# Two loops over groups unrolled into single streams of products, and rows of maxima moved in one transfer

## The chip, the cores and the metric

The kernel runs on one core of a Trainium2 chip. The metric is the device time of one execution in microseconds (us). Three runs of the kernel before took 4997.11, 5010.97 and 5019.95 us; the median is 5010.97 us.

## What is computed

The program is a chain of eight blocks over 4096 tokens of width 128 (16 sequences of 256), each with a residual and a layer norm: an encoder of six attention layers, a mixture of experts, a gated delta rule, an FP4 network, a linear attention, a ternary network, an attention with rotary positions, and a Fourier mix. The change touches the encoder, the experts, the ternary network and the rotary attention. Cut to what matters, the reference of the two networks is:

```python
# experts: every token goes through the shared network and all 8 experts; the gates are zero but for the top 2
shared = silu(x @ shared_w1.T) @ shared_w2.T                    # 128 -> 512 -> 128
logits = x @ gate_w.T                                           # 8 per token
gates  = scatter(softmax(top_k(logits, 2)))
expert_out = einsum('teh,edh->ted', silu(einsum('td,ehd->teh', x, experts_w1)), experts_w2)
out = shared + einsum('ted,te->td', expert_out, gates)          # then x + out, layer norm

# ternary network: _tlin(x, w, s) = (x @ w.T) * s, weights in {-1, 0, 1}
h = silu(_tlin(x, w1)) * _tlin(x, w2)                           # 128 -> 512
h = gelu(_tlin(h, h1)); h = gelu(_tlin(h, h2))                  # 512 -> 512, twice
out = _tlin(h, w3)                                              # 512 -> 128, then x + out, layer norm
```

In both attentions a softmax over 256 keys is taken for 16 heads of width 8. Its row maxima have to be known before the second pass over the scores; they are split into three bf16 pieces and enter that pass as three more rows of the product's operand.

## The kernel before, in words

The activations live in one array `H`, width on 128 partitions and 4096 tokens along it, worked in 8 groups of 512 tokens (`GROUP`, `GROUPS`). Blocks run one after another; each first loads its weights (`par_s<-par_in_s`). Every engine has its own stream of instructions, written out by hand in each block's `@block.tensor`, `.vector`, `.scalar`, `.gpsimd` and `.sync` function; semaphores join them, and nothing reorders them.

**Experts** (lines 1583 to 1723). All engines loop over the groups with `Fori`, so a group is begun when the last one is done. GpSimd copies the group from `H` to `cur` (L92). TensorE makes the 8 gate logits of each token (L1631, four small products), then for the shared network and each of 8 experts `up(e)` (L1640: four products of 512 columns into four banks) and `down(e)` (L1653: 16 products of 128 columns; for e = 0 four more, L1650, that add the residual by way of the identity), in the order up(0), up(1), down(0), up(2), down(1), ... down(8). ScalarE takes the SiLU of each `up` (L1717), VectorE adds each `down` with its gate (L1702). Then comes the norm, with a shared set of buffers: statistics on VectorE (L42 to L50), the root on GpSimd (L68), the scaling on VectorE (L56), four transposes on TensorE (L76, `norm_tensor`), the copy to `H` on ScalarE (L84), and with that the next round's copy to `cur`.

**Ternary network** (lines 2315 to 2403), likewise: per group 8 products for the two inputs' matrices (L2351, L2352), 16 and 16 for the two hidden layers (L2364), 4 for the output (L2368), all of 512 columns, then the residual and norm as above with four transposes more (L2372). ScalarE holds one table of functions at a time: it takes SiLU for the first four and GELU for the next eight activations of a group.

**Maxima.** In the encoder one sequence (`u`) is attended at a time, in four rounds T = 0 to 3 of four heads each. VectorE reduces the scores of sequence u + 2 (L751) while sequence u is in its second pass (scores L479, exponential L892, values L490). In round 2 of sequence u the maxima of u + 1 are turned by TensorE (L467) and copied by ScalarE to `turned_max`, 48 rows (three pieces by 16 heads) of 256 bf16 values (L881). The SyncE queue then runs `row_of_maxima`: it waits for that copy, stores `turned_max` to DRAM (L293), waits for the store (`s_nms`), and loads it back as three rows of 4096 values behind the query pieces (L295). TensorE waits for it (`s_nml`) before the first product of sequence u + 1 (L479). The same queue also stores the query and key pieces of the group after next (L286, L289), which ScalarE's queue waits for before it issues their loads (L263, L265). There are 96 such moves in the encoder and 16 in the rotary attention, where the lines are L1085 and L1087 and the product that waits is L1214.

Layer norms of the encoder and most blocks go through the class `Chain`, which has buffers of its own for each instance, and whose parts (`move`, `statistics`, `root`, `apply`, `turn`, `back`) are called apart.

## Time and profile before

| | |
|---|---|
| runs of the kernel before | 4997.11, 5010.97, 5019.95 us |
| profiled execution, its own time | 5029.85 us |
| its span, first to last instruction | 5027.8 us |
| TensorE matmul busy | 3880.8 us (77%) |
| TensorE weight load busy | 2644.1 us (53%) |
| VectorE busy | 2797.8 us (56%) |
| ScalarE busy | 1896.4 us (38%) |
| GpSimd busy | 786.3 us (16%) |
| mean granted TensorE clock | 0.861 |
| data moved by DMA | 224.83 MB, 45 GB/s |

The profiled execution ran 0.4% longer than the median of the runs. Busy shares are means over eight blocks with different limits; by time of the span the encoder lies at 0 to 2257 us, the experts at 2258 to 2878, the ternary network at 4219 to 4614, and the rotary attention from there to about 4970. The granted clock is the share of TensorE's full clock of 2.4 GHz that was let through: 1.00, or 0.50 at the lower level.

### The profile page before, as it was taken

The numbers are of one execution on the slowest core, as the hardware profiler recorded it, in microseconds if no ns is written. First come the engines' busy times: TensorE is split into PE (matmuls) and PEld (weight loads), VectorE is DVE, ScalarE is ACT, GpSimd is POOL, SyncE is SP. The second block draws the span as 40 slices with busy tenths as digits, with TensorE's granted clock in tenths as the row PEclk, the third lists the DMA queues.
The fourth block names the chain that finished last, engine by engine and source line by source line (L and its number), as shares of the span: only waits on it lengthen the run. The fifth ranks groups of instructions, "written<-read, shape, count | busy, mean of one in ns | idle before, by whom it ended". The sixth has DMA issues, their size and how long they took to land. (4 is left out here: it accounts for less than half of the span.)

```text
span 5027.8 us, 72866 instructions
## 1 busy us (share of the span) xinstructions
PE 3880.8 (77%) x27543; PEld 2644.1 (53%) x27543; DVE 2797.8 (56%) x6776; ACT 1896.4 (38%) x2957; POOL 786.3 (16%) x1074
## 2 busy tenths in 40 slices
PE   5898888888888888868898744477745566887986
PEld 3666666666666666656666511155423332333664
DVE  4756656746746647551212277788679773111663
ACT  2554554554545545533333233322212122221343
POOL 2212222222222122130000000000000031002221
PEclk8999999998999899988999866589857677998897
DMA  5414414423424324200000000000000000001431
GB/s 124 101 36 107 105 42 100 106 53 90 95 49 114 74 61 112 75 10 29 0 0 0 13 0 0 0 1 1 1 5 0 4 1 23 0 0 34 105 86 32
DMA packets 158830, 224.83 MB, mean 45 GB/s; under 512 B 17950, under 2 KB 138142, under 8 KB 141214
## 3 DMA queue, kind: packets, MB, share of 16 engines
q10 hardware_dynamic: 19656, 107.37, 9.7%
q1 hardware_dynamic: 138878, 113.45, 8.3%
q8 instruction: 193, 3.16, 0.3%
q14 instruction: 103, 0.84, 0.1%
HBM read 157.18 MB, written 63.57 MB: 44 GB/s over the span
## 5 line engine op out<-in xcount | busy, mean ns | idle before, releaser
L751 DVE TENSOR_REDUCE enc_mx<-psum 128x2 f32<-128x512 f32 (+1 forms) x1152 | 753.2, 686 | 408.4 <-PE psum L460 404.1
L892 ACT ACTIVATE enc_e<-psum 128x1024 f32<-128x1024 f32 (+1 forms) x768 | 580.7, 808 | 506.6 <-PE psum L479 446.5
L460 PE MATMUL psum<-enc_ks,enc_qs 80*128 80x128 bf16 (+1 forms) x3072 | 469.2, 259 | 126.0 <-DVE enc_mx L751 110.8
L479 PE MATMUL psum<-enc_qs,enc_ks 83*128 83x256 bf16 (+1 forms) x3072 | 393.2, 255 | 95.6 <-DMA enc_qs<-max_pieces 87.2
L460 PEld LDWEIGHTS psum<-enc_ks,enc_qs 80*128 80x128 bf16 x3072 | 224.6, 102 | 268.9 <-DVE enc_mx L751 174.6
L490 PE MATMUL psum<-enc_e,enc_v 128*32 128x256 f32 (+1 forms) x6144 | 347.7, 346 | 0.0
L479 PEld LDWEIGHTS psum<-enc_qs,enc_ks 83*128 83x128 bf16 x3072 | 263.1, 101 | 145.7 <-DMA enc_qs<-max_pieces 101.5
L1653 PEld LDWEIGHTS psum<-par_s,moe_act_h 128*128 128x128 f32 x2304 | 268.6, 192 | 26.8 <-issue 26.8
L1640 PE MATMUL psum<-cur,par_s 128*128 128x512 f32 x576 | 275.2, 625 | 0.0
L1717 ACT ACTIVATE moe_act_h<-psum 128x512 f32<-128x512 f32 x288 | 169.4, 598 | 273.5 <-PE psum L1640 272.9
L1653 PE MATMUL psum<-par_s,moe_act_h 128*128 128x128 f32 x2304 | 271.5, 275 | 0.0
L1702 DVE SCALAR_TENSOR_TENSOR moe_acc<-psum,moe_gates,moe_acc 128x128 f32<-128x128 f32 x256 | 72.1, 345 | 352.4 <-PE psum L1653 352.4
L490 PEld LDWEIGHTS psum<-enc_e,enc_v 128*32 128x32 f32 x6144 | 165.5, 112 | 170.6 <-ACT enc_e L892 53.3
L169 POOL TENSOR_TENSOR enc_n_rstd<-enc_n_vareps,minus_half 128x4 f32<-128x4 f32 x112 | 114.1, 1019 | 897.9 <-DVE enc_n_vareps L165 888.7
L2364 PE MATMUL psum<-ter_h,par_s 128*128 128x512 f32 x512 | 221.0, 592 | 0.0
L548 PE MATMUL psum<-par_layerr,enc_hidden 128*128 128x128 f32 x1536 | 211.3, 283 | 0.0
L548 PEld LDWEIGHTS psum<-par_layerr,enc_hidden 128*128 128x128 f32 x1536 | 195.2, 199 | 0.0
L1359 DVE TENSOR_REDUCE rope_mx<-psum 128x2 f32<-128x512 f32 (+1 forms) x192 | 131.2, 690 | 99.8 <-PE psum L1198 96.9
L534 PE MATMUL psum<-H,par_layerr 128*128 128x512 f32 x384 | 173.6, 595 | 0.0
L1640 PEld LDWEIGHTS psum<-cur,par_s 128*128 128x128 f32 x576 | 110.9, 202 | 117.9 <-issue 112.3
L151 ACT ACTIVATE enc_n_rows<-psum 128x512 f32<-128x512 f32 x96 | 57.3, 597 | 301.0 <-PE psum L548 187.2
L174 DVE TENSOR_SCALAR enc_n_normed<-enc_n_rows,enc_n_meanvar,enc_n_rstd 128x128 f32<-128x128 f32 x384 | 152.2, 451 | 26.5 <-POOL enc_n_rstd L169 25.7
(452 smaller groups left out, 7498.6 us busy)
## 6 DMA issues: line engine op xcount, KB each, us to landing
enc_qs<-q_pieces ACTq DMA_DIRECT2D x234, 192.0 KB
enc_ks<-k_pieces ACTq DMA_DIRECT2D x234, 192.0 KB
k_pieces<-enc_pieces SPq DMA_DIRECT2D x240, 128.0 KB, 2.0
q_pieces<-enc_pieces SPq DMA_DIRECT2D x144, 128.0 KB, 2.0
enc_qs<-q_pieces SPq DMA_DIRECT2D x54, 192.0 KB
enc_ks<-k_pieces SPq DMA_DIRECT2D x54, 192.0 KB
rope_qs<-q_pieces ACTq DMA_DIRECT2D x39, 192.0 KB
rope_ks<-k_pieces ACTq DMA_DIRECT2D x39, 192.0 KB
```

Of the source, the lines that this page charges most:

```text
L174: last = self.c.nc.vector.tensor_scalar(self.normed[:, t, :], self.rows[:, t, :], self.meanvar[:, t, 0:1], self.rstd[:, t:t + 1], ALU.subt ...
L460: last = T_.matmul(p1[f % 2][:, i * kw:(i + 1) * kw], qs[0:KEYED, slot, h, j * P:(j + 1) * P], ks[0:KEYED, slot, h, 0:kw], start=True, sto ...
L479: last = T_.matmul(p2[ch][:, g], ks[0:SCORED, slot, 4 * T + g, ch * P:(ch + 1) * P], qs[0:SCORED, slot, 4 * T + g, 0:n], start=True, stop= ...
L490: last = T_.matmul(o[T // 2][32 * g:32 * g + 32, T % 2, 0:n], v[:, u % SLOTS, ch, 4 * T + g], e_of(T, ch)[:, g], start=(ch == 0), stop=Tru ...
L534: T_.matmul(up_bank[f], LR["w1"][:, f * P:(f + 1) * P], c.H[:, grp(g)], start=True, stop=True).then_inc(s_h, 1)
L548: last = T_.matmul(down_bank[:, sl], hidden[:, g % 2, f, sl], LR["w2"][:, f * P:(f + 1) * P], start=False, stop=(f == 3))
L751: V.tensor_reduce(mx[:, u % 2, j * HEADS + h0:j * HEADS + h0 + n], p1[f % 2].rearrange("p (h k) -> p h k", h=n), AX_X, ALU.max)\
L892: A.activation(e_of(T, ch), p2[ch], ACT.Exp, scale=HD ** -0.5).then_inc(s_e, 1)
L1640: nc.tensor.matmul(c.bank[1 + f], W["w1"][:, at:at + P], c.cur[:], start=True, stop=True).then_inc(s_h, 1)
L1653: last = nc.tensor.matmul(b[:, sl], act_h[:, e % 2, f, sl], W["w2"][:, at:at + P], start=(f == 0 and e > 0), stop=(f == FC - 1))
L1717: nc.scalar.activation(act_h[:, e % 2, f], c.bank[1 + f], ACT.Silu).then_inc(s_silu, 1)
L2364: last = nc.tensor.matmul(bank[5 + f % 2], wt[:, kk, f * P:(f + 1) * P], src[:, kk], start=(kk == 0), stop=(kk == FC - 1))
```

## The change

The experts and the ternary network are written without `Fori`, as one stream per engine over all groups, in which the next group's first products are put ahead of the last group's norm.

- Experts: the products read `H` itself, so `fetch_group` and `cur` go. `up(n + 1)`, `down(n)` runs on over the groups' borders (n counts 72 networks of 8 groups). The gate logits of group g + 1 are made after `down` of network 1 of group g (`choose`), its ranks after network 3 on VectorE, its gates after network 6. The norm of group g - 1 is done inside group g: statistics after network 0, scaling after network 1, transposes after network 3, the copy to `H` with the gate's exponential after the SiLUs of network 5 on ScalarE. Two sets of accumulators, gates and `Chain` buffers alternate.
- Ternary network: the input products of group g + 1 are put between the hidden layers of group g (two pairs) and behind them (two pairs); the transposes of group g - 1 stand behind the first product sum of hidden layer 1 (`rows`) and the second of hidden layer 2 (`turn`). `Chain` replaces the shared norm, and its `move` copies the rows from PSUM to SBUF (one more activation a group). ScalarE now changes between SiLU and GELU four times a group instead of twice.
- Both take semaphores of their own, cleared behind a barrier of all engines at the end of the block.
- Maxima: one transfer from `turned_max` to the three rows of `qs`, without DRAM and without the wait for the store, in the encoder and the rotary attention.

```diff
@@ -290,10 +290,7 @@
 
             def row_of_maxima(layer, nxt, u):
                 sp.wait_ge(s_nmm, at(layer, 16, u + 1, nxt))
-                sp.dma_start(c.params["max_pieces"][u % 2], turned_max[:]).then_inc(s_nms, 16)
-                sp.wait_ge(s_nms, at(layer, 256, 16 * (u + 1), nxt))
-                sp.dma_start(qs[KEYED:SCORED, u % SLOTS].rearrange("p h q -> p (h q)"),
-                             c.params["max_pieces"][u % 2].rearrange("(a h) c -> a (h c)", h=HEADS)).then_inc(s_nml[u % 2], 16)
+                sp.dma_start(qs[KEYED:SCORED, u % SLOTS].rearrange("p h q -> p (h q)"), turned_max[:]).then_inc(s_nml[u % 2], 16)
 
             def first(layer, nxt):
                 store(layer, nxt, 0)
...
+            def choose(g):
+                if g:
+                    pe.wait_ge(s_gate, GATE * (g - 1) + 1)
+                for t in range(TILES):
+                    last = T_.matmul(bank[7][:, t * EXPERTS:(t + 1) * EXPERTS], c.H[:, tile_of(g, t)], W["gate"], start=True, stop=True)
+                last.then_inc(s_logit, 1)
+
+            def up(n):
+                g, e = n // E1, n % E1
+                for f in range(FC):
+                    if n:
+                        pe.wait_ge(s_silu, (n - 1) * FC + f + 1)
+                    at = (e * FC + f) * P
+                    T_.matmul(bank[1 + f], W["w1"][:, at:at + P], c.H[:, grp(g)], start=True, stop=True).then_inc(s_h, 1)
+
+            def free(n):
+
+                g, e = n // E1, n % E1
+                if e == EXPERTS:
+                    pe.wait_ge(N[g % 2].s_moved, g // 2 + 1)
+                else:
+                    pe.wait_ge(s_acc, g * EXPERTS + e + 1)
+
+            def down(n):
+                g, e = n // E1, n % E1
+                pe.wait_ge(s_silu, (n + 1) * FC)
+                if n >= 2:
+                    free(n - 2)
+                b = bank[5 + n % 2]
+                for t in range(TILES):
+                    sl = slice(t * P, (t + 1) * P)
+                    if e == 0:
+                        T_.matmul(b[:, sl], c.H[:, tile_of(g, t)], c.ident, start=True, stop=False)
+                    for f in range(FC):
+                        at = (e * FC + f) * P
+                        last = T_.matmul(b[:, sl], act_h[:, n % 2, f, sl], W["w2"][:, at:at + P], start=(f == 0 and e > 0), stop=(f == FC - 1))
+                last.then_inc(s_down, 1)
+
+            def turn(g):
+                if g:
+                    pe.wait_ge(N[(g - 1) % 2].s_done, (g - 1) // 2 + 1)
+                N[g % 2].turn(pe, g // 2, bank[0])
...
-            with pe.Fori(0, GROUPS) as i:
-                pe.wait_ge(c.s_cur, i + (base + 1))
...
-                up(0)
-                for e in range(1, E1):
-                    up(e)
-                    down(e - 1)
-                down(E1 - 1)
-                norm_tensor(c, pe, i + base)
+            choose(0)
+            up(0)
+            for n in range(RUNS):
+                g, e = n // E1, n % E1
+                if n + 1 < RUNS:
+                    up(n + 1)
+                down(n)
+                if e == 1 and g + 1 < GROUPS:
+                    choose(g + 1)
+                if e == 3 and g:
+                    turn(g - 1)
+            turn(GROUPS - 1)
...
+                if e == 0 and g:
+                    N[(g - 1) % 2].statistics(dve, (g - 1) // 2)
+                if e == 1 and g:
+                    if g >= 3:
+                        dve.wait_ge(N[(g - 1) % 2].s_turned, (g - 1) // 2)
+                    N[(g - 1) % 2].apply(dve, (g - 1) // 2)
+                if e == 3 and g + 1 < GROUPS:
+                    rank_experts(g + 1)
+                if e == 6 and g + 1 < GROUPS:
+                    weigh(g + 1)
...
+            gate_exp(0)
+            for n in range(RUNS):
+                g, e = n // E1, n % E1
+                if n >= 2:
+                    act.wait_ge(s_down, n - 1)
+                for f in range(FC):
+                    act.wait_ge(s_h, n * FC + f + 1)
+                    A.activation(act_h[:, n % 2, f], bank[1 + f], ACT.Silu).then_inc(s_silu, 1)
+                if e == 5 and g:
+                    back(g - 1)
+                if e == 5 and g + 1 < GROUPS:
+                    gate_exp(g + 1)
+            back(GROUPS - 1)
...
+            def up(g, f):
+                n = FC * g + f
+                if n >= 2:
+                    pe.wait_ge(s_h0, n - 1)
+                T_.matmul(bank[1 + f % 2], W["w1"][:, f * P:(f + 1) * P], c.H[:, grp(g)], start=True, stop=True)
+                T_.matmul(bank[3 + f % 2], W["w2"][:, f * P:(f + 1) * P], c.H[:, grp(g)], start=True, stop=True).then_inc(s_up, 1)
+
+            def hidden(g, layer, f):
+                n = 2 * FC * g + layer * FC + f
+                wt = W[("h1", "h2")[layer]].rearrange("p (k n) -> p k n", k=FC)
+                if f == 0 and layer == 0:
+                    pe.wait_ge(s_h0, FC * (g + 1))
+                elif f == 0:
+                    pe.wait_ge(s_g, n)
+                if n >= 2:
+                    pe.wait_ge(s_g, n - 1)
+                for k in range(FC):
+                    src = h1[:, k] if layer else h0[:, g % 2, k]
+                    last = T_.matmul(bank[5 + f % 2], wt[:, k, f * P:(f + 1) * P], src, start=(k == 0), stop=(k == FC - 1))
+                last.then_inc(s_p, 1)
+
+            def rows(g):
+                pe.wait_ge(s_sum, g + 1)
+                if g:
+                    pe.wait_ge(N[(g - 1) % 2].s_done, (g - 1) // 2 + 1)
+                for t in range(TILES):
+                    last = T_.transpose(bank[0][:, t * P:(t + 1) * P], y[:, g % 2, t * P:(t + 1) * P], c.ident)
+                last.then_inc(N[g % 2].s_rows, 1)
+
+            def turn(g):
+                N[g % 2].turn(pe, g // 2, bank[0])
+
             W.wait(pe)
-            with pe.Fori(0, GROUPS) as i:
...
+                for f in range(FC):
+                    hidden(g, 1, f)
+                    if f == 1 and g:
+                        turn(g - 1)
+                for f in range(2, FC):
+                    if g + 1 < GROUPS:
+                        up(g + 1, f)
+                pe.wait_ge(s_g, 2 * FC * (g + 1))
+                if g:
+                    pe.wait_ge(s_sum, g)
+                for k in range(FC):
+                    last = T_.matmul(bank[7], W["w3"][:, k * P:(k + 1) * P], h2[:, k], start=(k == 0), stop=(k == FC - 1))
                 last.then_inc(s_y, 1)
-                pe.wait_ge(s_sum, i + 1)
-                for t in range(TILES):
-                    last = nc.tensor.transpose(bank[1][:, t * P:(t + 1) * P], y[:, t * P:(t + 1) * P], c.ident)
-                last.then_inc(s_rows, 1)
-                norm_tensor(c, pe, i + base)
+            rows(GROUPS - 1)
+            turn(GROUPS - 1)
...
+                    gelu(g, 0, f)
+                    if f == 1 and g:
+                        move(g - 1)
+                for f in range(2):
+                    if g + 1 < GROUPS:
+                        gate(g + 1, f)
+                for f in range(FC):
+                    gelu(g, 1, f)
+                    if f == 3 and g:
+                        back(g - 1)
+                for f in range(2, FC):
+                    if g + 1 < GROUPS:
+                        gate(g + 1, f)
+            move(GROUPS - 1)
+            back(GROUPS - 1)
```

The order of TensorE's instructions at the border from the first to the second group of the experts. Before (the rows at the end of the loop's body, after which it begins again at the gate logits, L1631):

```order
L1653 MATMUL psum<-par_s,moe_act_h 128x128 x16
L1643 REGISTER_ALU
L1645 REGISTER_ALU
L1653 MATMUL psum<-par_s,moe_act_h 128x128 x16
L76 MATMUL psum<-par_const,normed 128x128 x4
L1628 REGISTER_ALU
L1628 COMPARE_AND_BRANCH
```

In the changed kernel, where L1638 is `up`, L1660 `down`, L1657 the residual, L1629 the gate logits and L182 the norm's transposes, from the residual of the second group on:

```order
L1657 MATMUL psum<-par_const,H 128x128
L1660 MATMUL psum<-par_s,moe_act_h 128x128 x4
L1638 MATMUL psum<-H,par_s 128x512 x4
L1660 MATMUL psum<-par_s,moe_act_h 128x128 x16
L1629 MATMUL psum<-par_s,H 128x8 x4
L1638 MATMUL psum<-H,par_s 128x512 x4
L1660 MATMUL psum<-par_s,moe_act_h 128x128 x16
L1638 MATMUL psum<-H,par_s 128x512 x4
L1660 MATMUL psum<-par_s,moe_act_h 128x128 x16
L182 MATMUL psum<-par_const,moe_n_normed 128x128 x4
L1638 MATMUL psum<-H,par_s 128x512 x4
```

The transposes stood behind the group's last `down` with nothing after them but the branch; now they stand behind network 3 of the next group, with products on both sides.

TensorE in the ternary network, before, the end of the loop's body:

```order
L2364 MATMUL psum<-ter_h,par_s 128x512 x4
L2368 MATMUL psum<-ter_h,par_s 128x512 x2
L2367 REGISTER_ALU
L2368 MATMUL psum<-ter_h,par_s 128x512
L2367 REGISTER_ALU
L2368 MATMUL psum<-ter_h,par_s 128x512
L2370 REGISTER_ALU
L2372 MATMUL psum<-par_const,ter_y 128x128 x4
L76 MATMUL psum<-par_const,normed 128x128 x4
L2346 REGISTER_ALU
L2346 COMPARE_AND_BRANCH
```

Changed, where L2408 and L2409 are the input products, L2422 the hidden layers, L2458 the output, L2430 and L182 the two sets of transposes:

```order
L2458 MATMUL psum<-ter_h,par_s 128x512 x4
L2422 MATMUL psum<-ter_h,par_s 128x512 x4
L2430 MATMUL psum<-par_const,ter_y 128x128 x4
L2422 MATMUL psum<-ter_h,par_s 128x512 x12
L2408 MATMUL psum<-H,par_s 128x512
L2409 MATMUL psum<-H,par_s 128x512
L2408 MATMUL psum<-H,par_s 128x512
L2409 MATMUL psum<-H,par_s 128x512
L2422 MATMUL psum<-ter_h,par_s 128x512 x8
L182 MATMUL psum<-par_const,ter_n_normed 128x128 x4
```

Behind the output products (L2458) the next group's hidden layer now follows at once, and both sets of transposes have moved into it.

The SyncE queue in the encoder, before:

```order
L293 DMA max_pieces<-enc_turned_max 48x256
L295 DMA enc_qs<-max_pieces 3x4096
L293 DMA max_pieces<-enc_turned_max 48x256
L295 DMA enc_qs<-max_pieces 3x4096
L286 DMA q_pieces<-enc_pieces 128x2x256 x3
L289 DMA k_pieces<-enc_pieces 128x2x256 x5
```

Changed, the same stretch:

```order
L293 DMA enc_qs<-enc_turned_max 3x16x256 x2
L286 DMA q_pieces<-enc_pieces 128x2x256 x3
L289 DMA k_pieces<-enc_pieces 128x2x256 x5
```

Two sequences' maxima take two transfers instead of four, and the stores of the pieces stand behind one of them instead of behind a store, a wait and a load.

## Rows read from the trace of the kernel before

**Rows 1.** Experts: us, busy of PE, PEld, DVE, ACT, POOL, PEclk, DMA share, GB/s.

```profile
2500.00:2600.00 100.00, 93.25 (x491) 66.09 (x492) 20.56 (x76) 34.48 (x57) 1.67 (x3) 0.92 0.00 0
```

**Rows 2.** Waits of TensorE over the span: us in total, times, longest us.

```profile
PE psum L479 <- DMA enc_qs<-max_pieces: 87.2, 56, 4.4
PE psum L76 <- DVE normed L56: 74.1, 16, 5.1
PE psum L1214 <- DMA rope_qs<-max_pieces: 14.5, 7, 4.4
```

**Rows 3.** Timeline of the experts: start us, duration us, engine, line, instruction [idle <-releaser].

```profile
2334.73 6.53 PE L1653 MATMUL psum<-par_s,moe_act_h 128*128 128x128 f32 x57
...
2348.99 1.88 PE L1631 MATMUL psum<-par_s,cur 128*128 128x8 f32 x8 [1.57 <-POOL cur L92]
...
2359.74 0.38 PE L1650 MATMUL psum<-par_const,cur 128*128 128x128 f32 x2
...
2364.20 3.60 PE L1640 MATMUL psum<-cur,par_s 128*128 128x512 f32 x8
...
2371.21 3.60 PE L1640 MATMUL psum<-cur,par_s 128*128 128x512 f32 x8
...
2409.68 7.31 PE L1653 MATMUL psum<-par_s,moe_act_h 128*128 128x128 f32 x64
...
2422.06 1.09 PE L76 MATMUL psum<-par_const,normed 128*128 128x128 f32 x4 [5.08 <-DVE normed L56]
...
2424.70 1.88 PE L1631 MATMUL psum<-par_s,cur 128*128 128x8 f32 x8 [1.55 <-POOL cur L92]
...
2863.48 7.31 PE L1653 MATMUL psum<-par_s,moe_act_h 128*128 128x128 f32 x64
```

**Rows 4.** 5 us behind a border of two groups of the experts, columns as in Rows 1.

```profile
2425.00:2430.00 5.00, 5.00 (x13) 2.93 (x13) 2.80 (x10) 0.83 (x3) 0.00 (x0) 0.50 0.00 0
```

**Rows 5.** Timeline of the ternary network, the same columns.

```profile
4264.88 3.60 PE L2368 MATMUL psum<-ter_h,par_s 128*128 128x512 f32 x8
4269.31 0.66 PE L2372 MATMUL psum<-par_const,ter_y 128*128 128x128 f32 x4 [0.84 <-DVE ter_y L2386]
...
4285.46 27.63 PE L2364 MATMUL psum<-ter_h,par_s 128*128 128x512 f32 x64
...
4286.37 1.28 ACT L2401 ACT_TABLE_LOAD   x1
...
4312.93 3.60 PE L2368 MATMUL psum<-ter_h,par_s 128*128 128x512 f32 x8
...
4603.22 3.60 PE L2368 MATMUL psum<-ter_h,par_s 128*128 128x512 f32 x8
```

**Rows 6.** Timeline at the end of the encoder.

```profile
2256.71 0.60 ACT L933 ACTIVATE H<-psum 128x512 f32<-128x512 f32 x1 [4.26 <-PE psum L182]
2258.54 0.36 SPq L2971 DMA_DIRECT2D par_s<-par_in_s  x1
```

**Rows 7.** Timeline of the encoder, a sequence's maxima from store to use.

```profile
825.29 0.32 SPq L293 DMA_DIRECT2D max_pieces<-enc_turned_max  x1
...
828.52 0.25 SPq L295 DMA_DIRECT2D enc_qs<-max_pieces  x1
...
830.65 0.61 PE L479 MATMUL psum<-enc_qs,enc_ks 83*128 83x256 bf16 x4 [2.60 <-DMA enc_qs<-max_pieces]
```

**Rows 8.** Waits of the SyncE queue, and the store L293 by itself (issue to landing).

```profile
SPq L295 <- DMA max_pieces<-enc_turned_max: 212.5, 96, 4.2
```

```profile
DMA to landing us min/median/max: 1.4/2.7/4.5
```

**Rows 9.** 2 us behind waits for the maxima in the encoder, columns as in Rows 1.

```profile
106.00:108.00 2.00, 2.00 (x18) 0.62 (x18) 0.78 (x2) 0.90 (x2) 0.00 (x0) 0.50 0.01 4
...
2082.00:2084.00 2.00, 2.00 (x13) 1.94 (x12) 1.38 (x2) 1.44 (x2) 0.00 (x0) 0.50 0.00 0
```

298 lines of the change are left out of this document (154 added, 144 removed).

## The prediction

> **What bounds the kernel now.** I read the busy time by stretches of the span first, then TensorE's waits, then the timeline where the change works. In the experts TensorE is busy 93% of a stretch at a mean clock of 0.92, the others a third or less [rows 1]: products bound it, and what is missing lies at the borders of the groups. The waits name three places that the change touches: the encoder's second pass for the maxima, 87.2 us in 56 waits; the same in the rotary attention, 14.5 us in 7; and the shared norm's transposes in both networks, 74.1 us in 16 [rows 2].
>
> **Experts.** The last `down` of a group ends 7.31 us after 2409.68, at 2416.99; the transposes start at 2422.06, the next gate logits at 2424.70 [rows 3]. So 7.7 us pass between the last product of a group and the first of the next, of which the transposes are about 1. Then TensorE runs at its lower level, 0.50, for the next 5 us [rows 4], and the gate logits take 1.88 us. A period is 2424.70 - 2348.99 = 75.71 us.
>
> In the changed order a group costs only its products. One network is 2371.21 - 2364.20 = 7.01 us, nine are 63.1. The residual's four products lengthen network 0: from 2359.74 to 2364.20 is 4.46 us, and a plain `down` is half of the 7.31 that two take, less the last product's end, 3.57: 0.9 more. Four transposes at full clock are 0.66 [rows 5]. The gate logits are between half of 1.88 and 1.88; I take 1.2, nearer to the half since the clock stays up. Together 65.9 us. From the end of the first group's products, 2341.26, to that of the last, 2870.79 [rows 3], the seven periods took 529.5 us; seven of 65.9 are 461. That is 68 us.
>
> This holds if nothing else is late. VectorE's work on one network is small, and `down(n)` needs the sum of network n - 2, which has two `up` and a `down` (3.4 + 3.6 + 3.4 us) to be made; the ranks or statistics beside it are 2 to 3 us. ScalarE's insertion after network 5 is a copy of 0.6 us, two changes of table at 1.28 [rows 5] and the small exponential, about 3.4 us, against a `down` of 3.6 during which it has no SiLU to take. If that cover failed by a microsecond, it would cost 7 us in all.
>
> **Ternary network.** The output products of the first group start at 4264.88, of the last at 4603.22 [rows 5]: 338.3 us for seven periods of 48.3. In the changed order a period is 32 hidden products in 4312.93 - 4285.46 = 27.5 us (0.858 each), 4 for the output 3.4, 8 input products 6.9 and two sets of transposes 1.3 [rows 5], 39.1 us. Group 0 takes up the second group's input products (6.9), groups 1 to 6 cost 39.1 each, group 7 32.2 without them: 273.7 us. That is 65 us less.
>
> ScalarE changes its table four times a group, 5.1 us. Each change has a cover: two pairs of input products (3.4 us) come before the next hidden layer, and I follow it so: table 1.28, SiLU 0.7, SiLU by 4.3 us after the hidden layer's end, table by 5.6, first GELU wanted at 6.9. VectorE's norm (some 4 us with GpSimd's root) lies beside a hidden layer of 13.7 us. If one change in each group came 1.3 us late, that would be 9 us.
>
> **Block ends.** The encoder, which already has a barrier and clears its semaphores, shows 1.2 us from its last activation's end (2257.31) to the next block's first transfer [rows 6]. Two blocks get this, and `move` adds an activation to the last norm: 3 us more, at most 4, not below 0.
>
> **Maxima.** The old way has two legs: the store, issued at 825.29 and seen by the queue at 828.52, and the load from there until TensorE starts at 830.65, 3.2 and 2.1 us [rows 7]. The store took 1.4 us when the queues were quiet, 2.7 in the middle, 4.5 at most, and the queue waited 212.5 us for its 96 [rows 8]. TensorE's 56 waits were 0.2 to 4.4 us long. The new single transfer has no row. Its bounds: as quick as the quiet store, 1.4 us, so that over 3 us go and nearly the whole 87.2 us; or as slow as both legs together, so that nothing goes. A loss would need it slower than both (below). I take it as long as the store at its place, since it has the store's 48 pieces of 512 B and meets the same traffic; the load's 2.1 us go. Of 56 waits of 87.2 us together, cutting each by up to 2.1 leaves about 8, so 79 us; the rest of TensorE's path behind them moves up in full only if VectorE keeps pace, and I count nine tenths, 71 us. If the transfer comes out half a microsecond longer than the store, it is 62. In the rotary attention 14.5 us in 7 waits become 10 us of gain by the same cut.
>
> The Trainium skill, "DMA: Bandwidth & Descriptors", section on why a DMA increments its semaphore by 16, says that a transfer is spread over the largest number of engines up to 16 that divides the outermost dimension of both sides. By it the store (48 and 48 rows) uses 16 engines, the load and the new transfer (3 rows on one side) use 3. That speaks against taking the new one for a second store: it would resemble the load, 2.1 us or somewhat more in traffic. The same page's account of one DMA puts most of the fixed cost, some 2 us, on the receipt of the write, with DRAM the slowest target, and speaks for the new one. By the first rule alone what goes is the store leg, whose median is above the load's, and the sum would be some 80 us rather than 71.
>
> Behind such a wait TensorE also falls to 0.50 [rows 9]. I find 14 such stretches of 3.4 or 6.8 us next to waits for the maxima (the first and the last of them are shown), 61 us at half clock, which can cost at most half of that, 30 us. Some of them have waits for VectorE beside them that stay; I take 12, with 0 and 30 as ends. The stores of the pieces are issued about 1.2 us sooner in every second sequence, since the queue no longer waits for the maxima's store; ScalarE's loads behind them come sooner too. I count this as nothing: TensorE seldom waits for it.
>
> **Sum.** 68 + 65 - 3 + 71 + 10 + 12 = 223 us. The profiled execution took 5029.85 us and would take 4807. The median of the runs, 5010.97 us, is 0.4% lower; with the same gain it becomes 4788, which I predict.
>
> **Rivals.**
>
> *The single transfer is no faster than the two.* Then the waits [rows 2] and the stretches at 0.50 stay, and only 68 + 65 - 3 = 130 us go: 4881 us. For it: no transfer from SBUF to SBUF stands in the trace, and 48 small pieces into 3 rows may be slow. Against: the whole DRAM round with its second issue goes. 11 in 100.
>
> *The streams get new waits.* ScalarE's table changes or VectorE's inserted norms come late at every border: 1 us at four places in each of 16 groups would be 64 us, half of that 32. The sum goes to 4820. Against: the slack worked out above is positive everywhere, if at places under a microsecond. 10 in 100.
>
> *More than counted goes.* Both ends at their best: 87 + 14 + 30 + 68 + 65 - 3 = 261 us, 4750 us. 12 in 100.
>
> *Slower: the transfer into three rows is long.* Place: TensorE's first product of each of 112 sequences. Every microsecond beyond the old way's mean of about 4.8 us (the queue's wait 212.5/96 = 2.2 and its issue 0.3, then the load's 2.1 or a little more) is paid by the 63 sequences that waited, in the end by all 112. To undo 130 us it needs 1.2 to 2.1 us more, so 6.0 to 6.9 us a transfer; at 8 us it costs 63 x 3.2 = 202 us and more, and the time is some 5083 us. Against: the longest store was 4.5 us [rows 8]. 2 in 100.
>
> The forecast's own case has 65 in 100, between about 4760 and 4815 us. The range reaches to the first rival's edge: 4742 to 4850. Faster by over 0.5% (25 us, about what a measurement of this kernel tells from no change): 0.97. Within 0.5%: 0.01. Slower: 0.02.
>
> **What would show it.** In the changed profile the experts and the ternary network have TensorE busy above 98% at a clock of 1.00 but for their first microseconds; 65 to 67 us lie between a group's residual products and the next group's; 39 to 40 us between two sums of output products in the ternary network. No wait for the norm's transposes is left in the two. The waits of the encoder's second pass for the maxima are under 20 us instead of 87.2, and the new transfer is seen 2 to 3 us before its product. The wait of VectorE's scores reduction for TensorE falls by nearly as much. The prediction is wrong if the waits stay with the new transfer as their releaser, or if they go and the waits for VectorE's reduction grow by as much.

## The result and the profile after

The changed kernel takes 4772.28 us (median of 4 runs, 4746.57 to 4779.46) beside 5004.85 us for the kernel before (4997.11 to 5019.95): a ratio of 0.952, 95% interval 0.9482 to 0.9557. On two further chips it was timed again, and gave 0.9484 (0.9459 to 0.9509) and 0.950 (0.947 to 0.9529). The forecast was 4788 us in a range of 4742 to 4850.

The profiled execution of the changed kernel took 4746.57 us, its span 4744.7 us, at a mean granted clock of 0.883 (0.861 before). I measure the blocks from one load of a block's weights to the next:

| us | before | after | difference | forecast |
|---|---|---|---|---|
| encoder | 2249.0 | 2114.4 | -134.6 | -83 |
| experts | 619.4 | 546.5 | -72.9 | -68 |
| ternary network | 395.7 | 333.8 | -61.9 | -65 |
| rotary attention | 351.8 | 337.4 | -14.4 | -10 |

The delta rule, the FP4 network, the linear attention and the Fourier mix stay within 2 us of where they were.

The busy time of 100 us in the experts, and of 5 us behind the last `down` of the first group (us, busy of PE, PEld, DVE, ACT, POOL, PEclk, DMA share, GB/s), answer to [rows 1] and [rows 4]:

```profile
2300.00:2400.00 100.00, 100.00 (x583) 73.59 (x582) 23.23 (x90) 38.94 (x64) 1.01 (x1) 1.00 0.00 1
...
2210.00:2215.00 5.00, 5.00 (x24) 3.09 (x23) 1.12 (x4) 2.39 (x4) 0.00 (x0) 1.00 0.00 0
```

TensorE is busy 100% at full clock where it was 93% at 0.92. Its timeline in the experts (start us, duration us), from the residual products (L1657) of one group to those of the next, answers to [rows 3]:

```profile
2213.79 0.38 PE L1657 MATMUL psum<-par_const,H 128*128 128x128 f32 x2
...
2225.26 0.96 PE L1629 MATMUL psum<-par_s,H 128*128 128x8 f32 x8
2226.07 3.68 PE L1638 MATMUL psum<-H,par_s 128*128 128x512 f32 x8
...
2240.17 0.60 PE L182 MATMUL psum<-par_const,moe_n_normed 128*128 128x128 f32 x4
```

```profile
2279.07 0.38 PE L1657 MATMUL psum<-par_const,H 128*128 128x128 f32 x2
```

A group takes 2279.07 - 2213.79 = 65.28 us, forecast 65.9. The gate logits take 2226.07 - 2225.26 = 0.81 us, forecast 1.2, and the transposes 0.6, with no idle time ahead of either. What is left of the old waits stands at the end of the block, where no products are left to cover the last norm:

```profile
2668.33 1.08 PE L182 MATMUL psum<-par_const,moe_n_normed 128*128 128x128 f32 x4 [5.15 <-DVE moe_n_normed L174]
```

The narrowest cover was ScalarE's, after network 5. Its timeline there:

```profile
2310.02 0.59 ACT L1755 ACTIVATE H<-psum 128x512 f32<-128x512 f32 x1
2310.63 1.28 ACT L1751 ACT_TABLE_LOAD   x1
2311.92 0.23 ACT L1751 ACTIVATE moe_weight<-moe_shifted 128x32 f32<-128x32 f32 x1
2314.00 1.28 ACT L1764 ACT_TABLE_LOAD   x1 [1.85 <-PE psum L1638]
2315.29 2.06 ACT L1764 ACTIVATE moe_act_h<-psum 128x512 f32<-128x512 f32 x4
```

The copy to `H`, the first change of table and the exponential fit. The second change does not start until the first product of the next `up` is there, so its 1.28 us come behind that product, and the four SiLUs then run back to back: they catch up by themselves. Only TensorE's weight loads show waits for them, 1.7 us in 7 places, and its products run on beside these, so they cost nothing.

In the ternary network, two sums of output products (L2458), which answer to [rows 5]:

```profile
4067.54 3.60 PE L2458 MATMUL psum<-ter_h,par_s 128*128 128x512 f32 x8
...
4074.40 0.60 PE L2430 MATMUL psum<-par_const,ter_y 128*128 128x128 f32 x4
...
4095.44 0.60 PE L182 MATMUL psum<-par_const,ter_n_normed 128*128 128x128 f32 x4
...
4106.18 3.60 PE L2458 MATMUL psum<-ter_h,par_s 128*128 128x512 f32 x8
```

38.64 us lie between them, forecast 39.1. At the block's two ends TensorE has short waits that no border inside has: 1.28 and 1.62 us for VectorE up to the first hidden layer, twice 0.78 us for ScalarE in the last group, and 4.59 us for the last norm. The encoder's waits of TensorE (us, times, longest), which answer to [rows 2]:

```profile
PE psum L457 <- DVE enc_mx L748: 108.9, 182, 1.6
...
PE psum L476 <- DMA enc_qs<-enc_turned_max: 15.5, 17, 3.3
```

Of 87.2 us, 15.5 are left. VectorE's reduction, which had waited 404.1 us for TensorE's scores, now waits 292.6.

### The profile page after: what moved, and what is told of

Same layout as the page of the kernel before. It is cut to its first block and busy times, and to the rows that moved or that the text cites. A ratio compares the mean times of both kernels' runs of the same rounds, so it can differ in the third digit from the quotient of the medians.

```text
span 4744.7 us, 71737 instructions
## 1 busy us (share of the span) xinstructions
PE 3758.3 (79%) x27543; PEld 2577.3 (54%) x27543; DVE 2783.0 (59%) x6776; ACT 1913.5 (40%) x2979; POOL 778.8 (16%) x1058
## 5 line engine op out<-in xcount | busy, mean ns | idle before, releaser
L748 DVE TENSOR_REDUCE enc_mx<-psum 128x2 f32<-128x512 f32 (+1 forms) x1152 | 749.8, 685 | 296.0 <-PE psum L457 292.6
L457 PE MATMUL psum<-enc_ks,enc_qs 80*128 80x128 bf16 (+1 forms) x3072 | 459.4, 255 | 124.9 <-DVE enc_mx L748 108.9
L476 PE MATMUL psum<-enc_qs,enc_ks 83*128 83x256 bf16 (+1 forms) x3072 | 383.9, 250 | 20.4 <-DMA enc_qs<-enc_turned_max 15.5
L487 PE MATMUL psum<-enc_e,enc_v 128*32 128x256 f32 (+1 forms) x6144 | 336.7, 338 | 0.0
L1660 PEld LDWEIGHTS psum<-par_s,moe_act_h 128*128 128x128 f32 x2304 | 269.7, 192 | 30.1 <-issue 28.5
L1660 PE MATMUL psum<-par_s,moe_act_h 128*128 128x128 f32 x2304 | 272.6, 275 | 0.0
L1638 PE MATMUL psum<-H,par_s 128*128 128x512 f32 x576 | 261.3, 597 | 0.0
L2422 PE MATMUL psum<-ter_h,par_s 128*128 128x512 f32 x512 | 224.9, 593 | 2.4 <-DVE ter_h L2473 1.6
L2858 PE MATMUL psum<-rule_against,par_s 128*128 128x256 f32 x256 | 98.0, 467 | 89.3 <-DVE rule_against L2897 89.3
```

The costliest lines, as they stand in the source:

```text
L457: last = T_.matmul(p1[f % 2][:, i * kw:(i + 1) * kw], qs[0:KEYED, slot, h, j * P:(j + 1) * P], ks[0:KEYED, slot, h, 0:kw], start=True, sto ...
L476: last = T_.matmul(p2[ch][:, g], ks[0:SCORED, slot, 4 * T + g, ch * P:(ch + 1) * P], qs[0:SCORED, slot, 4 * T + g, 0:n], start=True, stop= ...
L487: last = T_.matmul(o[T // 2][32 * g:32 * g + 32, T % 2, 0:n], v[:, u % SLOTS, ch, 4 * T + g], e_of(T, ch)[:, g], start=(ch == 0), stop=Tru ...
L748: V.tensor_reduce(mx[:, u % 2, j * HEADS + h0:j * HEADS + h0 + n], p1[f % 2].rearrange("p (h k) -> p h k", h=n), AX_X, ALU.max)\
L1638: T_.matmul(bank[1 + f], W["w1"][:, at:at + P], c.H[:, grp(g)], start=True, stop=True).then_inc(s_h, 1)
L1660: last = T_.matmul(b[:, sl], act_h[:, n % 2, f, sl], W["w2"][:, at:at + P], start=(f == 0 and e > 0), stop=(f == FC - 1))
```

## The experiments

Each kernel was timed beside runs of the kernel before on the same chip, and its ratio is to those. A range in brackets is the 95% interval.

**One part at a time.** *e1_maxima*: the kernel before, with the single transfer of the diff in the encoder and the rotary attention and nothing else.

> Only the maxima's transfer is changed, in the encoder and the rotary attention. Theory (the waits are on the path and the parts add up): the whole change gained 233 us by the runs and the two networks' share by the profiles' stages is 73 + 62 = 135, so this alone gives about 98 us less, 4905 to 4915 where the kernel before takes 5005; the encoder's waits for the maxima fall from 87 to about 15 us. Rival (most of the encoder's 135 us in the two profiled executions is luck of the granted clock, which fell less often in the one than in the other): 65 to 80 us less, and TensorE's clock in the encoder no better than before. The forecast's own terms said 71 + 10 + 12 = 93.

4905.94 us, ratio 0.9797 (0.9766 to 0.9829), 108 us less than the 5014.3 beside it. The waits for the maxima are 14.3 us in 18. The gain's interval, 86 to 117 us, holds the theory's 98 and leaves the rival's 65 to 80 out.

*e2_experts*: the kernel before with the new experts alone.

> Only the experts are one stream of products. Theory: seven borders of 9.9 us and the clock behind them go, less a barrier: 67 to 74 us less than before, about 4935. Rival (part of it is given back in the blocks before or behind): under 60 us.

4951.19 us, 0.9889 (0.9855 to 0.9923), 63 us less (39 to 73). The block is 547.2 us long, as in the whole change. The interval holds both the theory and the rival; it is the block's length that speaks for the theory.

*e3_ternary*: the new ternary network alone.

> Only the ternary network is one stream. Theory: 60 to 65 us less than before, about 4943. Rival (the table changes and the moved norm cost something at each border that the profile of the whole hid): under 55 us.

4960.85 us, 0.9902 (0.987 to 0.9935), 53.5 us less (33 to 65). By its median this is the rival's side, under 55, but the block is 335.1 us long and so 60.6 us shorter, and the other blocks behind the encoder are within 4 us of where they were, so nothing is seen to be given back. The three parts sum to 225 us, each known to some 16 us, and the whole gave 233, 250 and 260 in its three timings: within that they add.

*e4_no_loop*: the kernel before, where both networks' `Fori` are written out and no instruction is moved.

```diff
-            with pe.Fori(0, GROUPS) as i:
+            for i in range(GROUPS):
```

> The kernel before with the loops over groups of the experts and the ternary network written out and nothing moved: the same instructions in the same order, without register arithmetic and branches. Theory (the order is what counts: the norm's chain and the clock's fall behind it): within 5 us of before, since only the branch, some tenths of a us at each of 14 borders, goes. Rival (the loops' branches and the waits on register values cost at each border): 15 us or more less than before.

5014.97 us, 0.9997 (0.9973 to 1.0021). The waits for the norm's transposes are 74.1 us in 16, to the tenth those of [rows 2]. The two blocks are 616.5 and 393.0 us long, 2.9 and 2.7 us less than before, of the 135 that the change takes off them. So the gain of the two networks is the order of the products, not the loops' branches. No run moves GpSimd's copy, the gate or the norm alone.

**What a transfer costs.** *e5_after_again*: the changed kernel on the chip of the three that follow.

> The changed kernel again, on the chip of the next three. If the parts add up (108 + 63 + 53 = 224 us by the medians of the kernels with one part each), it takes some 225 to 235 us less than the kernel before.

4761.65 us, 0.9484 (0.9459 to 0.9509): 260 us less, somewhat more than expected.

*e6_twice*: the changed kernel with two legs again, neither of which touches DRAM.

```diff
-  sp.dma_start(qs[KEYED:SCORED, u % SLOTS]..., turned_max[:]).then_inc(s_nml[u % 2], 16)
+  sp.dma_start(between[:, u % 2], turned_max[:]).then_inc(s_nms, 16)
+  sp.wait_ge(s_nms, at(layer, 256, 16 * (u + 1), nxt))
+  sp.dma_start(qs[KEYED:SCORED, u % SLOTS]..., between[:, u % 2]).then_inc(s_nml[u % 2], 16)
```

> The changed kernel with the maxima moved in two transfers again, but by way of a spare tile in SBUF instead of DRAM, with the queue's wait between them. Theory (what gained is the shorter path, which saves both waits and falls of the clock): the waits for the maxima come back to 80 us or more, TensorE's time at half clock in the encoder goes from 203 to 240 us back to about 310, and the kernel takes 85 to 110 us more than the changed one. Rival (DRAM was what was slow, the number of legs is not): the first leg is under 1.4 us in quiet and the kernel is less than 40 us behind the changed one.

4983.95 us, 0.9916 (0.9892 to 0.9939): 222 us above e5_after_again, twice what was expected and twice what e1_maxima had won. The sequence shown in [rows 7], here:

```profile
830.68 0.55 SPq L294 DMA_DIRECT2D enc_between<-enc_turned_max  x1
...
832.88 0.78 SPq L296 DMA_DIRECT2D enc_qs<-enc_between  x1
...
835.65 1.04 PE L479 MATMUL psum<-enc_qs,enc_ks 83*128 83x256 bf16 x4 [1.87 <-DMA enc_qs<-enc_between]
```

The second leg takes 835.65 - 832.88 = 2.8 us, where the load from DRAM took 2.1, and the two issues take 0.55 and 0.78 us of the queue, where they took 0.32 and 0.25. The first leg's landing:

```profile
DMA to landing us min/median/max: 1.7/2.3/4.5
```

That is beside 1.4/2.7/4.5 into DRAM [rows 8]. The encoder's waits are 123.2 us in 63. So it is not DRAM that had made the old way slow: two legs within SBUF are slower than the two through DRAM, and the change wins because it has one leg. The difference in time is small, though. From the issue of the first leg to that of the second there are 2.48 us in the mean, where DRAM had 2.54, and from there to a product that waited 2.77 us, where it had 2.26: half a microsecond more in all. With it the encoder has 36 us more of waits than before the change and 100 us more at half clock (431.1 against 330.8). Why the clock fell for so much longer is open. The Trainium skill, "DMA: Bandwidth & Descriptors", section on latency, says that the receipt of the write dominates a transfer's fixed cost and that DRAM is the slowest target. This run agrees in the median (2.3 against 2.7) and not in the quiet case (1.7 against 1.4).

*e7_three*: the changed kernel, its transfer cut into three, 16 rows into one row each.

```diff
+  for a in range(3):
+      sp.dma_start(qs[KEYED + a:KEYED + a + 1, ...], turned_max[a * HEADS:(a + 1) * HEADS]).then_inc(s_nml[u % 2], 16)
```

> The changed kernel with one transfer for each of the three rows: 16 rows of turned_max into one row of the operand, three issues instead of one. Theory (a transfer with 3 rows on one side goes by 3 engines, each with 16 pieces of 512 B one after another, which is why the new transfer takes 2.7 us and more to its product): with 16 rows against 16 pieces all engines share it, the last of the three issues comes 0.6 us later, the time from the first issue to the product stays about 2.7 us in quiet and is shorter in traffic; waits for the maxima 8 to 15 us, time within 10 us of the changed kernel. Rival (the number of pieces or the one row they go into sets the time): 0.6 us longer each, waits over 22 us, 10 to 20 us more.

4800.99 us, 0.9556 (0.9531 to 0.9581), 39 us above e5_after_again. The waits rise to 40.4 us in 38. One of them, the three issues and the product that waits:

```profile
798.92 1.98 SPq L294 DMA_DIRECT2D enc_qs<-enc_turned_max  x3
```

```profile
803.64 0.61 PE L477 MATMUL psum<-enc_qs,enc_ks 83*128 83x256 bf16 x4 [1.41 <-DMA enc_qs<-enc_turned_max]
```

Over the sequences where TensorE waited, there are 3.07 to 5.5 us from the first of the three issues to its product, median 3.95. With the single transfer of e5_after_again it is 2.65 to 4.1 us, median 3.47. So the split makes the hand-over half a microsecond longer, as the rival said, and costs twice what it said. From the last of the three issues it is 1.89 to 3.95 us, median 1.96: each transfer of 8 KB is over sooner than the one of 24 KB, but the last is issued 1.2 us or more behind the first. Whether the smaller size or more engines make it quicker, no run tells apart.

**The clock at a border.** *e8_filler*: the kernel before, with five products that nobody reads behind a group's last `down`.

```diff
+  for f in range(5):
+      nc.tensor.matmul(c.bank[1], W["w1"][:, f * P:(f + 1) * P], c.cur[:], start=True, stop=True)
```

> The kernel before with five more products of 512 columns at the end of each group of the experts, behind the last down and ahead of the wait for the norm; their results are never read. They fill 4.3 of the 5.1 us in which TensorE sits idle and change nothing else, so any gain is the clock's. Theory (the low level behind a border costs 3 us of the 9.9): the gate logits take about 1 us instead of 1.9 and the first products run at full clock, 8 groups make 15 to 25 us less than before. Rival (the remaining idle time for ScalarE's and GpSimd's copies lets the clock fall anyway, or the clock costs nothing): within 5 us of before.

5020.37 us, 0.9992 (0.9974 to 1.001), so within the rival's 5 us. TensorE and ScalarE at a border:

```profile
2430.60 4.46 PE L1663 MATMUL psum<-cur,par_s 128*128 128x512 f32 x10
2435.84 0.63 PE L76 MATMUL psum<-par_const,normed 128*128 128x128 f32 x4 [0.79 <-DVE normed L56]
2437.22 1.28 ACT L1713 ACT_TABLE_LOAD   x1
2438.03 1.06 PE L1631 MATMUL psum<-par_s,cur 128*128 128x8 f32 x8 [1.56 <-POOL cur L92]
2438.95 3.68 PE L1640 MATMUL psum<-cur,par_s 128*128 128x512 f32 x8
2442.08 1.28 ACT L1719 ACT_TABLE_LOAD   x1
2444.03 3.70 PE L1640 MATMUL psum<-cur,par_s 128*128 128x512 f32 x8 [1.40 <-ACT moe_act_h L1719]
```

At this border the granted clock stayed at 1.00, where it was 0.50 in [rows 4], and the gate logits take 1.06 us instead of the 1.88 of [rows 3]. At others it fell all the same. Behind this border and behind the second one after it (columns as in [rows 4]):

```profile
2438.00:2443.00 5.00, 4.59 (x16) 2.33 (x16) 3.23 (x12) 1.65 (x3) 0.00 (x0) 1.00 0.00 0
...
2588.00:2593.00 5.00, 5.00 (x12) 3.04 (x13) 2.70 (x9) 0.83 (x3) 0.00 (x0) 0.50 0.00 0
```

Of the seven borders only two kept the clock, and the time at half clock in the block went from 97 to 56 us. So the filler did a part of its work only. Where the clock held, the group behind it took 74.05 us; where it fell, 75.5 to 75.7, and before mostly 75.3. The block is 616.4 us long instead of 619.4. Where it held, TensorE is sooner through its first `up` and then waits 1.40 us for ScalarE. ScalarE's second table load, for the SiLU, can't start before its exponential, and that waits for VectorE, which works 2.7 us on the logits first; the first table load is over before the logits are made. So about half of what a held clock gives at a border is spent again in this chain. The theory's 15 to 25 us is neither shown nor refuted for a clock held everywhere: two borders suggest 1.3 us each. In the changed kernel the gate stands inside the last group, which takes this chain away as well.

**Shorter or earlier?** TensorE's waits before stand mostly behind transfers issued in even sequences: 46 of 56, 65.7 us. Three kernels ask whether it would have been enough to ask for the maxima a round earlier. *e9_earlier*: the changed kernel with that in the odd sequences (the same edit on VectorE, and on ScalarE for `move_max`).

```diff
                         if T == 1 and odd:
...
-                            masked_sum(layer, u)
-                        if T == 2 and u + 1 < SEQS:
+                            if u + 1 < SEQS:
+                                turn_max(layer, 0, u + 1)
+                        if T == 2 and odd:
+                            if u + 1 < SEQS:
+                                pe.wait_ge(s_nmm, at(layer, SEQS, u + 2))
+                            masked_sum(layer, u)
+                        if T == 2 and not odd and u + 1 < SEQS:
```

> The changed kernel, but in every second sequence (odd u) of the encoder the maxima of the next sequence are turned by TensorE and copied by ScalarE one round earlier (T = 1 instead of T = 2); the masked sum that stood there goes to T = 2. The single transfer then has about two rounds of four heads more of time, in 48 of the 96 sequences. The changed kernel shows 15 to 16 us of waits for the maxima in 17 to 19 places. Theory (what is left of those waits and a part of the stretches at half clock comes from a transfer asked for too late): the waits fall below 6 us, some 10 to 25 us go, ratio to the changed kernel 0.995 to 0.998. Rival (the waits that are left belong to the even sequences, or VectorE's maxima are not ready a round earlier, so TensorE and ScalarE wait for them instead): the waits move to VectorE as releaser and the time stays within 10 us or grows.

4712.44 us, 0.9398 (0.9371 to 0.9426): the fastest kernel of the study, 52 us below the changed one on its chip, twice the theory. Its waits:

```profile
PE psum L457 <- DVE enc_mx L750: 82.7, 155, 1.6
...
PE psum L476 <- DMA enc_qs<-enc_turned_max: 9.3, 13, 3.3
```

The transfer's waits gave only 5 us of it. What fell too are the waits of the first pass for VectorE, 107.0 us to 82.7, those for the encoder's norms (L182), 42.0 to 34.5, and the time at half clock, 251.8 to 174.2. The reason I had for this kernel was nearly wrong; that it won twice what I expected is luck. The edit also moves VectorE's scaling of the masked sum from a round that has the norm's statistics and a normalisation to one that has the norm's scaling instead; that this is the cause is argued, not shown, as no run moves it alone.

*e10_dram_early*: the same edit, but the maxima still by way of DRAM.

> The old way of the maxima (store to DRAM, wait, load) in encoder and rotary attention, the new streams in experts and ternary network, and the earlier turn of e9_earlier in the odd sequences of the encoder. It asks whether the waits could have been hidden instead of made shorter. Without the earlier turn this mixture would stand some 105 us above the changed kernel (e1_maxima). Theory (the waits come from how late the transfer is asked for, and odd and even sequences share them): the 88 us of waits fall to about half, 35 to 50 us, with the clock's part 50 to 60 us in all are won back, so the time is 45 to 60 us over the changed kernel. Rival (waits are nearly all behind even sequences, where nothing is moved): 90 to 110 us over. Other rival (nearly all behind odd ones): under 25 us over.

4838.95 us, 0.9642 (0.9613 to 0.9672), 74 us over the changed kernel: between the theory's 45 to 60 and the first rival's 90 to 110, and neither's mechanism. The waits for the maxima are 90.2 us in 70, no less than before; VectorE's fell to 83.3.

*e11_after_third*, the changed kernel on this chip:

> The changed kernel again, on the chip of e9_earlier and e10_dram_early. Both theories: ratio to the kernel before 0.945 to 0.955. Encoder length = 2010 + waits for the maxima + 0.45 x us at half clock, as in the eight profiles so far: within 10 us of it.

4764.52 us, 0.950 (0.947 to 0.9529). Its encoder is 2131.0 us long, 6.5 us under the rule that was expected of it. The same rule is 25 and 18 us too long for e9_earlier and e10_dram_early.

*e12_dram_both*: e10_dram_early with the turn a round earlier in the even sequences as well.

```diff
-                        if T == 1 and not odd and m + 2 < GROUPS:
+                        if T == 1 and not odd:
                             pe.wait_ge(s_masked, at(layer, SEQS, u + 1))
-                            project(layer, 0, m + 2, 1, misc)
+                            turn_max(layer, 0, u + 1)
```

> e10_dram_early (maxima by way of DRAM) with the earlier turn in the even sequences too: the maxima of u + 1 are turned and copied in round 1, the second product of the projection and its ScalarE and VectorE parts go to round 2. In the profile of the kernel before, 46 of the 56 waits, 66.7 of 88 us, stand behind transfers issued in even sequences (those of an odd u + 1), which e10_dram_early did not move, and its waits stayed (90.2 us in 70). Theory (these waits come from how late the even sequence asks, and can be hidden): waits fall under 40 us, the time falls by 40 to 80 us against e10_dram_early, ratio to the kernel before 0.948 to 0.957, so a DRAM round asked for earlier is worth about what the single transfer is. Rival (GpSimd's cutting of the maxima or the queue of stores sets when the transfer can start, not TensorE's turn): waits stay above 70 us and the time within 15 us of e10_dram_early, 0.961 to 0.968, or above it since the pieces come a round later.

4819.8 us, 0.9585 (0.9559 to 0.9611). By the ratios this is 0.6% or 29 us below e10_dram_early, with intervals that just don't meet: less than the theory's 40 to 80 us and more than the rival's 15. The waits are 70.8 us in 66. The queue and the store's landing show why asking earlier brings so little:

```profile
818.51 0.32 SPq L293 DMA_DIRECT2D max_pieces<-enc_turned_max  x1
...
824.48 0.25 SPq L295 DMA_DIRECT2D enc_qs<-max_pieces  x1
```

```profile
SPq L295 <- DMA max_pieces<-enc_turned_max: 404.1, 96, 6.2
```

```profile
DMA to landing us min/median/max: 1.4/5.0/6.5
```

The store is issued a round sooner and lands later: median 5.0 us instead of 2.7 [rows 8], and the queue waits 4.2 us for it instead of 2.2. It now starts 2.4 us behind the last of ScalarE's six loads of pieces for a later sequence (issued from 814.12 to 816.11, 192 KB each); at the same place before it was 4.06 us, and nowhere under 3. Sorted by that distance (from issue to issue), the time from the store's issue to that of the load behind it is:

| store issued behind the last load by | before: count, median us | e10_dram_early | e12_dram_both |
|---|---|---|---|
| under 3 us | 0 | 36, 5.21 | 73, 5.18 |
| 3 to 4.5 us | 23, 3.42 | 6, 3.78 | 4, 4.54 |
| 4.5 to 6 us | 49, 2.65 | 30, 2.10 | 1, 2.85 |
| 6 to 12 us | 6, 1.69 | 6, 2.15 | 0 |
| over 12 us | 18, 1.40 | 18, 1.40 | 18, 1.40 |

In all three kernels the same store takes 1.40 us far from the loads and more the closer it comes to them. The early turn moves 36 and 73 of the 96 stores right behind them, and much of the time that it gains is spent there. That the loads are the cause is read from this sorting; no run moves the loads alone.

## Why the prediction was right, and where it was not

**Experts: right.** The period was forecast 65.9 us and is 65.28; seven of these, 4 us, are the difference between 68 and 72.9. The run with this part alone gives 63 (39 to 73). No cover failed.

**Ternary network: right.** 65 forecast, 61.9 by the profiles, 53.5 (33 to 65 by its interval) by the run with it alone. From the first to the last output products (4067.54 to 4333.17) the profile has 265.6 us, 72.7 less than in [rows 5]; my working had 273.7, mostly since it put the second group's input products (6.9 us) into this interval, though they stand ahead of it. They cost there: the stretch from the block's weights to the first output products grew by 9.8 us, these 6.9 and two new waits for VectorE, 2.9 together.

**The waits for the maxima: right in size, partly by luck.** 87.2 less 15.5 is 71.7 us, forecast 71. Behind it two errors cancel. I took the transfer to be as long as a store at its place, took the load's 2.1 us off each wait and so had 79 us of waits go, of which I counted nine tenths as time. The transfer is longer: its product comes 3.3 us after its issue in the mean, of which 0.7 are the issue itself, so fewer waits went. And VectorE kept pace (TensorE's waits for it are 108.9 us, 110.8 before), so nothing had to be taken off what went. Over the sequences in which TensorE waited, the old way took 4.8 us in the mean from the store's issue to the product, so 1.4 us went: less than the load's 2.1, and less than the store leg's 2.5, which is the other reading that the prediction gave. Its term of some 80 us was no nearer. Its reason, the number of engines, is neither shown nor refuted by e7_three, where the smaller transfers are quicker one by one and three issues cost more than that.

**The clock: the mis-sized term.** The prediction took 12 us with 30 as the upper end. The encoders of fourteen profiles say more. Four numbers are enough for its length: TensorE's waits for the maxima, its waits in the first pass for VectorE, and the us at half clock (over stretches of 2 us, twice the clock's shortfall from 1.00 times the length).

| encoder, us | length | waits, maxima | waits, VectorE | at half clock | by the rule |
|---|---|---|---|---|---|
| before | 2249.0 | 87.2 | 110.8 | 330.8 | 2247 |
| e4_no_loop | 2248.2 | 88.0 | 107.0 | 338.1 | 2247 |
| e3_ternary | 2213.5 | 82.5 | 110.0 | 253.6 | 2207 |
| e6_twice | 2326.0 | 123.2 | 110.0 | 431.1 | 2327 |
| after | 2114.4 | 15.5 | 108.9 | 203.2 | 2116 |
| e5_after_again | 2118.7 | 16.0 | 108.8 | 220.1 | 2124 |
| e11_after_third | 2131.0 | 14.2 | 107.0 | 251.8 | 2135 |
| e7_three | 2163.6 | 40.4 | 101.2 | 234.4 | 2147 |
| e9_earlier | 2072.6 | 9.3 | 82.7 | 174.2 | 2070 |
| e10_dram_early | 2193.1 | 90.2 | 83.3 | 245.5 | 2184 |
| e12_dram_both | 2163.5 | 70.8 | 86.1 | 223.6 | 2158 |

The rule is 1900 + both waits + 0.45 x the us at half clock, fitted to these. It had no term for VectorE's waits until e9_earlier and e10_dram_early missed it, and in this form it has foretold no run: it describes these encoders. All fourteen but e7_three lie within 10 us of it (three are left out of the table), and e7_three is 17 above. The kernels with the old transfer and the old order have 254 to 349 us at half clock, mean 318, those with the new one 203 to 252, mean 229: 89 us of half clock go, worth 40 by the rule. The runs say less: their medians fell by 233, 260 and 250 us on the three chips, and less the 221 us of the other terms (72.9, 61.9, 71.7 and 14.4) that leaves 12, 39 and 29. So the prediction's 12 is at the low end of what the runs show, and the term is not known better than to 12 to 40 us. I had counted only the stretches right behind a wait for the maxima, 61 us, and most of them at less than their half. The low clock that went is more than the stretches that I could pin to those waits, and 0.45 us paid for each us of it is nearly the half that it can cost at most.

e3_ternary warns against reading one profile too closely: its encoder is the old one, word for word, and is 35 us shorter because its clock was better in that execution. The same is true of the 134.6 us in the first table, of which some 57 are clock where the mean is 40.

**Rotary attention and block ends: right.** 14.4 us for 10 forecast, of which 7.7 are waits for the maxima (14.5 to 6.8). From the last `down` or output product to the next block's weights the experts' end grew by 0.55 us and the ternary network's by 0.9, for 3 forecast. The sum of the profiles is 284 us in four blocks, for an execution that was the fastest of its kernel; the medians' difference is 233, near the 223 forecast.

**Signs named ahead.** Held: TensorE above 98% at full clock between the blocks' ends (100% and 99.3%); 65 to 67 us a group; waits for the maxima under 20 us; VectorE's waits down by 111.5. Missed: the transfer is issued 2.65 to 4.1 us before its product, not 2 to 3; a ternary group is 38.64 us, not 39 to 40; the transposes of the last norm still wait, 5.15 us in the experts and 4.59 in the ternary network.

**The rivals.** That the single transfer is no faster than two fell with e1_maxima. New waits did not come at the borders; 4.5 us of them stand at the ternary network's two ends. The slow transfer into three rows did not come either, but e6_twice shows that it was not absurd: there two legs that are together 0.5 us longer than the old way lose all that one had won. By the price that this rival gave, 0.5 us in 63 to 112 sequences would have cost 30 to 56 us; against the new streams with the old way, some 105 us over the changed kernel by e1_maxima, it cost about 115.

## What to carry to other kernels

Where groups of products bound a kernel and each ends in a norm, put the norm of the last group into the products of the next: what it gives is the period less the products' own time, and here it could be read off to 1% from rows of the kernel before, with every chain at the border (GpSimd's copy, the norm, and the gate with its table loads) moved away together. Look at every border before you say what a run shows: in e8_filler the clock held at two of seven. For a small dependent hand-over, count legs, not the memory that they pass. Before asking for a transfer earlier, look at what stands in the queues at that moment. And price a wait in front of a busy TensorE above its own length: with the 72 us of waits here some 90 us at half clock went, worth 40 us by the rule of the profiles and 12 to 39 by the runs.

## What the runs showed of the hardware that I had not expected

- A leg from SBUF to SBUF is hardly faster than one to or from DRAM with the same 24 KB. As a first leg it lands in 2.3 us in the median against 2.7, but in 1.7 against 1.4 at best; as the leg to the reader it takes 2.8 us against 2.1 to 2.6, and its issue holds the queue for 0.55 to 0.78 us against 0.25 to 0.32.
- A store of 24 KB takes 1.40 us to be seen by its queue with no load close ahead of it, 2.65 in the median at 4.5 to 6 us behind a train of loads of 192 KB, and 5.2 at under 3 us.
- Five products that fill 4.3 of 5.1 idle us at a border kept the clock at 1.00 at two of seven borders; at the other five it fell to 0.50 all the same.
- The spread of a kernel's runs goes with the clock that was granted: the changed kernel took 4746.57 us at a mean of 0.883 and 4779.46 at 0.874.
